# A four-part transformer kernel on one Trainium2 core: token sums moved to VectorE, one copy moved earlier, a key norm moved to GpSimd, and loops written out

## The reference

```
x = x + block_sparse_linear(layernorm(x))        # 512x512 weights, 32x32 blocks masked out, plus a bias
x = x + routed(layernorm(x))                     # 64 experts: softmax, top 8, their weights' sum times h, plus the mixed expert biases
x = x + attention(layernorm(x))                  # 32 query heads, 8 key heads of 128; keys and values through a latent of 32 per head; causal
x = x + feed_forward(layernorm(x))               # silu(h @ gate.T) * (h @ up.T) @ down.T, inner width 1376
```

## Time and profile before

| | |
|---|---|
| three runs | 1719.91, 1722.01, 1723.34 us; median 1722.01 |
| profiled execution | 1721.22 us by the device's clock, 1719.4 us from its first to its last instruction |
| busy share of the span | PE 96%, DVE 68%, ACT 55%, POOL 48% |
| mean granted PE clock | 0.99 of full speed |
| block 1 | from 0 to about 81 us |
| block 2 | to about 284 us (routing until about 165) |
| block 3 | to about 1358 us |
| block 4 | to 1719.4 us |

### The profile page before, as it was taken

How to read it: one execution, slowest core, us unless ns; L and a number is a source line. 1 busy time by engine, 2 the same in 40 slices (tenths; PEclk the granted TensorE clock), 3 DMA queues, 4 the chain that set the end, 5 groups by cost and what they waited for, 6 DMA issues and landing times. The chain is left out here.

```text
span 1719.4 us, 27002 instructions
## 1 busy us (share of the span) xinstructions
PE 1652.5 (96%) x8298; PEld 1375.8 (80%) x8298; DVE 1170.0 (68%) x3102; ACT 937.7 (55%) x2472; POOL 822.2 (48%) x1187
## 2 busy tenths in 40 slices
PE   5888999999999999999999999999999899999999
PEld 4667897788888888888888888888888678887887
DVE  7876425667767767767767767777777477866776
ACT  4476435556556657647657556656656343434432
POOL 4611002446346346346346346446446398747752
PEclk9979999999999999999999999999999999999999
DMA  5200455211111111124111111111110022003111
GB/s 157 77 1 1 181 200 208 74 38 50 62 38 50 62 38 49 62 87 172 62 38 50 62 38 42 60 47 38 51 61 26 31 64 72 32 25 123 50 49 49
DMA packets 61335, 114.94 MB, mean 67 GB/s; under 512 B 5457, under 2 KB 23889, under 8 KB 57105
## 3 DMA queue, kind: packets, MB, share of 16 engines
q1 hardware_dynamic: 60304, 112.74, 19.8%
q10 hardware_dynamic: 896, 0.56, 0.1%
HBM read 84.97 MB, written 28.31 MB: 66 GB/s over the span
## 5 line engine op out<-in xcount | busy, mean ns | idle before, releaser
L1773 PE MATMUL ps_q<-kv_w_hi,o_hi 128*128 128x512 f32 x512 | 205.7, 402 | 2.9 <-DVE o_lo L138 2.9
L1773 PE MATMUL ps_q<-kv_w_lo,o_hi 128*128 128x512 f32 x512 | 201.3, 393 | 0.0
L1773 PE MATMUL ps_q<-kv_w_hi,o_lo 128*128 128x512 f32 x512 | 201.0, 393 | 0.0
L138 POOL TENSOR_TENSOR kv_w_lo<-w_raw,kv_w_hi 128x512 fp32r<-128x512 f32 x128 | 163.1, 1291 | 58.0 <-ACT kv_w_hi L133 58.0
L1715 PE MATMUL ps_q<-h_hi,kv_w_hi 128*128 128x512 f32 x448 | 182.3, 407 | 3.0 <-PEq L1062 1.4
L1715 PE MATMUL ps_q<-h_hi,kv_w_lo 128*128 128x512 f32 x448 | 175.3, 391 | 0.0
L1715 PE MATMUL ps_q<-h_lo,kv_w_hi 128*128 128x512 f32 x448 | 175.2, 391 | 0.0
L133 ACT ACTIVATE kv_w_hi<-w_raw 128x512 fp32r<-128x512 f32 (+1 forms) x240 | 126.6, 566 | 64.6 <-POOL w_raw L479 62.1
L133 ACT ACTIVATE o_hi<-ps_o 128x512 fp32r<-128x512 f32 x128 | 76.2, 595 | 130.3 <-PE ps_o L1755 130.2
L1362 ACT ACTIVATE prob<-prob,neg_max 128x128 f32<-128x128 f32 x256 | 100.3, 392 | 84.2 <-DVE neg_max L1519 84.2
L1304 POOL TENSOR_SCALAR prob<-prob,inv_sum 128x128 f32<-128x128 f32 x256 | 95.2, 372 | 105.2 <-DVE inv_sum L1524 105.0
(11 more groups left out here) (237 smaller groups left out, 4890.3 us busy)
## 6 DMA issues: line engine op xcount, KB each, us to landing
w_raw<-in_wq_g SPq DMA_DIRECT2D x16, 1024.0 KB, 4.9
w_raw<-in_wo_g SPq DMA_DIRECT2D x16, 1024.0 KB, 4.8
k_scratch<-kv_stage SPq DMA_DIRECT2D x32, 256.0 KB, 2.5
v_scratch<-kv_stage SPq DMA_DIRECT2D x32, 256.0 KB, 2.1
k_raw<-k_scratch SPq DMA_DIRECT2D x32, 256.0 KB, 3.5
v_raw<-v_scratch SPq DMA_DIRECT2D x32, 256.0 KB, 3.8
f_gate_raw<-in_gate_c SPq DMA_DIRECT2D x10, 512.0 KB, 4.5
f_up_raw<-in_up_c SPq DMA_DIRECT2D x10, 512.0 KB, 3.7
```

Of the source, the lines that this page charges most:

```text
L138: return dve.tensor_tensor(parts[LO], src, parts[HI].bitcast(F32), ALU.subtract)
L1773: done = pe.matmul(ps_q[:, half, :], o[b][i][:, half, h, :], wo[j][:, h, :], start=(h == 0 and m == 0), stop=(h == GROUP - 1 and m == 2))
```

## The change

It has four parts.

- `skewed` has no hardware loop any more: all rounds are written out.
- In routing, `variance` of the key norm goes from DVE to POOL, and `h_next` is written by POOL (`apply`, a `tensor_scalar`) and no longer by ACT. DVE's `aggregate` waits for POOL's variance of two tiles before.
- `FeedTokens.sums` goes from POOL to DVE. For the first half it is spread over the end of DVE's `last_pair`; for the second half it stands at the head of `first_step(6)`.
- In the steps k = 1 and k = 7 of the feed forward, ACT's `copy("U", k)` comes right behind `given("G", k + 1)`, ahead of `gate.made_hi` and `down_part`. In the other steps it stays behind them.

```diff
-    if first is None:
-        first = depth + depth % 2 + 2
-    for i in range(first):
-        body(i, i % 2, lambda k, i=i: i - k >= 0)
-    with eng.Fori(first // 2, TILES // 2) as j:
-        for par in range(2):
-            body(2 * j + par, par, lambda k: True)
-    for i in range(TILES, TILES + depth):
-        body(i, i % 2, lambda k, i=i: i - k < TILES)
-        if tail:
+    for i in range(TILES + depth):
+        body(i, i % 2, lambda k, i=i: 0 <= i - k < TILES)
+        if tail and i >= TILES:
             tail(i - TILES)
...
     def pool_body(self, pool, i, par, live):
         if live(6):
+            self.ln_next.variance(pool, i - 6, par)
             self.ln_next.power(pool, i - 6)
+        if live(7):
+            t, odd = i - 7, (par - 1) % 2
+            if t >= 2:
+                pool.wait_ge(self.tn_done, t - 1)
+            self.ln_next.apply(pool, self.h_next[:, odd, :], tile_of(self.x, t), t).then_inc(self.h_next_done, 1)
...
-        if live(7):
-            t, pt = i - 7, odd
-            if not known(t) or t >= 2:
-                act.wait_ge(self.tn_done, t - 1)
-            self.ln_next.activate(act, self.h_next[:, pt, :], tile_of(self.x, t), t).then_inc(self.h_next_done, 1)
...
         if live(6):
+            if t6 >= 2:
+                dve.wait_ge(self.ln_next.ve_done, t6 - 1)
             self.ln_next.aggregate(dve, t6, par)
...
-        if live(6):
-            self.ln_next.variance(dve, t6, par)
...
                 up.single_lo(pool, 0, up_raw)
-                for j in range(4):
-                    feed.sums(pool, 0, j)
...
                     out_lo(u, 1, 0)
+                    feed.sums(dve, 0, 0)
                     add(u, 0, 1)
                     out_lo(u, 1, 1)
+                    feed.sums(dve, 0, 1)
+                    feed.sums(dve, 0, 2)
                     add(u, 1, 0)
+                    feed.sums(dve, 0, 3)
                     add(u, 1, 1)
...
-                    if k == WIDE:
-                        for j in range(4):
-                            feed.sums(pool, 1, j)
...
                         given("G", k + 1)
+                        if k % WIDE == 1:
+                            copy("U", k)
                         if (k + 1) % WIDE:
                             gate.made_hi(act, k + 1)
                     down_part(k)
-                    copy("U", k)
+                    if k % WIDE != 1:
+                        copy("U", k)
...
                 def first_step(k):
 
+                    if k:
+                        for j in range(4):
+                            feed.sums(dve, 1, j)
                     for pos in range(8):
                         turned(k // WIDE, 1, pos)
```

More of the change, by code:

```diff
@@ L628, in apply, with sums @@
         pool.tensor_scalar(self.tiles[j], self.x[:, t, :], self.ln.factor(t, 0), self.ln.factor(t, 1), ALU.mult, ALU.add).then_inc(self.h_done, 1)
-    def sums(self, pool, half, j):
+    def sums(self, dve, half, j):
         first, second = self.tiles[j], self.tiles[4 + j]
         n = 4 * (4 * half + j)
[L634 to L641, removed]
+        dve.wait_ge(self.t_done, self.flips(half, 0, 2 * j + 1))
+        dve.tensor_tensor(first[:, 0:2 * P], second[:, 0:2 * P], first[:, 0:2 * P], ALU.subtract).then_inc(self.made, 1)
+        dve.wait_ge(self.made, n + 1)
+        dve.tensor_tensor(second[:, 0:2 * P], second[:, 2 * P:4 * P], second[:, 0:2 * P], ALU.subtract).then_inc(self.made, 1)
+        dve.wait_ge(self.made, n + 2)
+        dve.tensor_tensor(second[:, 2 * P:4 * P], second[:, 2 * P:4 * P], first[:, 0:2 * P], ALU.subtract).then_inc(self.made, 1)
+        dve.wait_ge(self.made, n + 3)
+        dve.tensor_tensor(first[:, 2 * P:4 * P], first[:, 2 * P:4 * P], second[:, 2 * P:4 * P], ALU.subtract).then_inc(self.made, 1)
     def flip(self, pe, half, area, pos, bank):
```

## The result

The changed kernel takes 1710.62 us (median of 4 runs, 1709.74 to 1713.57), the kernel before 1720.96 us (median of 4, 1719.04 to 1723.34). The ratio is 0.9939, with a 95% interval of 0.9923 to 0.9954: 10.3 us faster. The profiled execution of the changed kernel is its slowest run, 1713.57 us with a span of 1711.8 us; the three others have spans of 1707.9 to 1708.9. Between the two profiled executions the span fell by 1719.4 - 1711.8 = 7.6 us, and it is these 7.6 us that the traces can explain.

The account below looks back on a forecast made before the run. PE, busy 96% of the span, bounds the kernel: only its work, clock and waits count. Terms 3.0 + 1.3 + 2.05 - 0.8 + 4.5 + 0.2 = 10.25 off 1721.2, plus 0.8 for the median, give 1711.7 us; 8-in-10 range 1708 to 1717.

Parts of the forecast that it names:

- Routing: Block 2: six rounds written out take 3.56 us each, 21.36 in place of 22.70; gain 1.3 us, bounds 1.0 to 1.6.
- step 6: Feed forward: sixteen sums behind DVE's last add make its first split 0.8 us late; loss 0.8, bounds 0.3 to 3.0.
- step 7: Feed forward: copy of P1 put ahead removes PE's 2.99 us wait and the low clock behind it; gain 4.5 us.
- step 1: Feed forward: the same move of the copy removes PE's other, small wait for it; gain 0.2 us.
- Block 1: Written-out loops: all rounds go at 3.205 us in place of 3.58; gain 3.0 us, bounds about 1.5 to 3.2.
- The rival: Loops and sums pay little: DVE and POOL overlap stays, sums on DVE run longer; 4.3 us won, 1717.4; chance 0.17.
- The move of the norm adds nothing: Routing: moving the norm gives no gain beyond the written-out rounds, since ACT is not far behind PE; 0 us.
- End of attention: Sums on DVE at 0.45 us each let PE start at 1356.9, not 1358.95; gain 2.05 us, range 1 to 2.6.
- Clock left low: Start of feed forward: PE's low clock stays in the forecast after 3.0 us idle; 2.15 us more if it stays up.
- The lower bound of 2.5: Feed forward, step 7: gain of only 2.5 us if a second wait takes part of the removed wait's place.
- The sum's second term: Feed forward, step 7: the low clock behind PE's wait, 0.57 over 3.6 us, also goes; 1.55 us.
- the slower rival: Routing's low clock lasts, 2.9 us more a round; from four more rounds the gain is gone, eight give 1735; chance 0.04.

Follow-up runs that it names:

- the one without sharing: Changed kernel with routing norm back on VectorE and ScalarE, second half's sums on GpSimd, first product piece ahead, first half's sums all on VectorE: 1708.73 us.
- the kernel with all four edits: Changed kernel with routing norm back on VectorE and ScalarE, second half's sums on GpSimd, first half's on both engines, first product piece ahead: 1703.48 us.

## Why the prediction came out right, step by step

The forecast was 1711.7 us and the median is 1710.6. But that agreement is partly luck: by its own sum the prediction had 10.25 us between the profiled executions, and there are 7.6. Routing, step 6 and step 7 were forecast too well and step 1 too low, each by over 0.5 us, and a higher mean clock in the other runs filled the difference.

- **Block 1, 3.0 us.** Measured 3.0 in the changed kernel's trace. The rival said that VectorE's and GpSimd's overlap makes the slow rounds and would stay. It didn't stay: writing out alone brings 3.2 us a round. But my reason against it was wrong. The written-out rounds hold the same two operations, yet not side by side: `kv_w_lo` takes 0.53 us in them, and the overlap itself comes with GpSimd's loop. What the loop costs in detail is shown in part: 1.84 of the 3.0 us hang on GpSimd's, none on VectorE's alone. Whether it is the register instructions, the branch or the overlap they bring wasn't separated. The Trainium skill's page "Runtime: NRT & Kernel Launch", section on instruction fetch mechanics, speaks of the branch; no run here tests it by itself.
- **Routing, 1.3 us.** Mis-sized: 0.5 measured. I took one round, 115.65 - 112.09, for the written-out pace; the pace is 3.67, as six rounds show. "The move of the norm adds nothing" was nearly right; it takes 0.17 us, and GpSimd's operation beside VectorE's small ones is the likely way.
- **End of attention, 2.05 us.** Measured 2.5, with 0.46 us a sum. The 0.04 us between links was right; the sums lie a little closer to the adds than I had them. "Clock left low" was wrong in its first part: the low clock came 0.3 us later and ended sooner than before, another 0.7 us.
- **Step 6, a loss of 0.8.** Mis-sized: 2.1 measured. 1.3 us is the gap itself (2.05 - 0.76), of which 0.95 came from one sum stretched beside GpSimd's remainder (1.37 for 0.42 us); the rest is the low clock behind it, of which PE's later waits gave some back. Both stood in the prediction as the upper bound and not in the sum. The same trace, with the sums back on GpSimd, has neither.
- **Step 7, 4.5 us.** The mechanism was right: P4 starts on time, and the wait and its low clock are worth 4.9 us by the account. The step that failed is the sentence "DVE, which stood with PE, then takes the other products as they come". It doesn't: it stands for a piece that ACT rounds behind the weights. Before, DVE waited for nothing else there, since it stood for P1's copy for 7.68 us anyway, and this hid it. The second wait took 2.9 us; what is left is 2.0. The lower bound of 2.5 held such a case, but not its size. The sum's second term, 1.55 us for the low clock, also hung on DVE: the run with the sums alone had the full clock behind the same wait and kept 0.1 us of it.
- **Step 1, 0.2 us.** 1.4 measured, at three places that each give 0.3 to 0.6 us: two small waits of PE (one for the copy, one for DVE's sum behind it), a later place where the profile shows no wait, and at each the slower first matmuls behind a stop. I had counted the first wait alone.
- **The rest.** The forecast left all other places as they were. In the profiled execution one of them, the attention's first scores, ran at the low clock and had not before, which cost 1.5 us at once, of which 1.1 came back where PE had waited before; all of the attention lost 0.5. In the other runs the clock was kinder: 0.992 against 0.990. The mean clock over the runs rose from 0.9887 to 0.9915, and 0.0028 x 1712 = 4.8 us of the 10.5 between the means (1721.7 over the 51 runs, 1711.1) come with that. The change removed the reasons for some of it (the clock behind step 7's wait, and part of that at the start); how much of the remaining is chance and how much the change's doing stays open, since the other runs have no trace. A slip in the rivals changes nothing: by its own terms the one in which loops and sums pay little is 1721.2 + 0.8 - 4.3 = 1717.7 us, not 1717.4.

## What to carry to other kernels

When a wait is removed, don't stop at what the waiting engine does next: look at the queue of the engine that released it, for each later instruction that somebody else needs. Here the copy was moved past the weights and the product piece was left behind them.

Take a pace from many rounds. One round out of ten was 0.1 us short, and that made the routing term almost three times too large.

Two engines that worked side by side on SBUF didn't add up here, and a busy engine's operation can be stretched by its neighbour just where it matters. And compare kernels that differ by a few us by the product of span and clock as well as by time, or where the clock happens to fall decides. Nor was the low clock's price a term of its own here: ask whether another engine would let PE use the full one.

## What the runs showed of the hardware

**Behind the same gap the clock falls in one execution and not in the next.** The 51 runs of the kernel before have mean clocks from 0.985 to 0.990, so it differs without any edit. Fourteen profiled executions (before, after and the twelve kernels above) have the same wait of PE ahead of the feed forward, 5.1 us long in five kernels and 2.2 to 2.6 us in nine. Behind 5.1 us the first matmul already has the low clock, in all five. Behind 2.2 to 2.6 us the first matmul always starts at full clock; in six of nine the clock falls when two to six matmuls have started and stays low for three to four microseconds, and in three it doesn't fall. In step 7 a wait of 2.5 to 3.7 us for P1's copy stands in five kernels; the low clock follows in four and not in the one shown above. Two kernels with the same gap to 0.01 us, the changed one (1353.20 us above, 0.57) and the one without sharing, show both:

```profile
1354.70:1358.70 4.00, 3.93 (x17) 3.28 (x18) 0.00 (x0) 0.84 (x1) 0.00 (x0) 1.00 0.51 148
```

**Routing's low clock ends in different rounds.** PE starts routing at half clock in all fourteen executions and is busy for 17.59 of the 21.30 us shown above, and yet the full clock returns only in the second, third or fourth of the rounds that hold `r_chosen`: the second in seven of the executions, the third in four, the fourth in three. Here is a window of an execution with the second, and one with the fourth:

```profile
79.00:98.50 19.50, 15.80 (x69) 12.42 (x68) 8.19 (x47) 10.40 (x24) 0.74 (x2) 0.58 0.00 0
```

```profile
79.60:106.00 26.40, 21.91 (x82) 16.52 (x81) 11.41 (x61) 13.62 (x32) 1.48 (x4) 0.50 0.00 1
```

The first is of the kernel with all four edits, the second of the one without sharing; by matching matmuls 4.3 of the 5.3 us between their spans arise there. The prediction gave four more rounds a chance of 0.04 as the slower rival. No such case came, but one more or one fewer is common, and it is worth as much as most of the edits.
